# Layer 1 of a two-layer graph network: node sums carried on TensorE by an identity product and copied by ScalarE, one-hots split between VectorE and ScalarE

## The reference

```python
h = jnp.maximum(_layernorm(x), 0.0)
h = (h @ W).reshape(n, 4, 64)
h_l, h_r = (a_l * h).sum(-1), (a_r * h).sum(-1)
e = h_l[row] + h_r[col]
e = jnp.where(e > 0, e, 0.2 * e)
m = segment_max(e, row)
ex = jnp.exp(e - m[row])
att = ex / (segment_sum(ex, row)[row] + 1e-16)
out = segment_sum(att[:, :, None] * h[col], row)
```

## Time and profile before

| | |
|---|---|
| time, median of three runs | 2322.39 us |
| profiled execution: its time, its span | 2321.69 us, 2319.9 us |
| busy share over the span: PE, DVE, ACT, POOL | 85%, 77%, 64%, 61% |
| granted TensorE clock, mean | 0.944 |
| layer 1: first and last maximum (L1297) | 1565.5 us and 2279.1 us |
| layer 1, 560 us from its middle: PE, DVE, ACT, POOL busy | 440.89, 509.18, 368.04, 380.02 us |

### The profile page before, as it was taken

The page is one execution under the profiler, slowest core; times in us unless marked ns, Lnnn a source line. Parts: engine busy times, 40 slices in busy tenths (PEclk is TensorE's granted clock), DMA queues, the critical chain, the costliest instruction groups (busy, mean ns, idle before and its releaser), DMA issues.

```text
span 2319.9 us, 42068 instructions
## 1 busy us (share of the span) xinstructions
PE 1961.0 (85%) x9839; PEld 1426.4 (61%) x9840; DVE 1784.6 (77%) x4372; ACT 1479.1 (64%) x5220; POOL 1409.6 (61%) x1393
## 2 busy tenths in 40 slices
PE   5999999999958899998988889837777877877874
PEld 3777777777747677777777777624444444544542
DVE  5655444444359999998999999667999989999987
ACT  1585555555567777777777777446666666666660
POOL 0377777666776666665666664247666666666660
PEclk9999999999989999999999999977999989998997
DMA  8534444333389888888889882034433333343311
GB/s 279 160 133 144 157 146 146 138 138 131 113 291 301 299 290 292 298 293 280 296 290 308 291 296 76 19 93 113 110 107 107 105 108 100 105 110 104 106 32 56
DMA packets 162185, 403.69 MB, mean 174 GB/s; under 512 B 46887, under 2 KB 59099, under 8 KB 162108
## 3 DMA queue, kind: packets, MB, share of 16 engines
q0 software_dynamic: 79360, 276.09, 36.8%
q1 hardware_dynamic: 82748, 126.67, 17.4%
HBM read 343.89 MB, written 84.72 MB: 185 GB/s over the span
## 4 chain that ended last, share of the span: by engine, by line
PE 39%; DVE 28%; issue 16%; DMA 8%; ACT 4%; DVEq 4%; POOL 2%; SPq 0%; ACTq 0%; POOLq 0%
PE ps L1405 15%; DMA arena<-sorted_edges 6%; DVE gmx L1297 5%; PE ps L1391 4%; PE ps L1518 3%; PE ps L1521 3%; DVE arena L1329 3%; PE ps L1456 3%; PE ps L1533 2%; DVE work L1292 2%; DVE sc L1139 2%; DVE arena L1125 2%; DVEq L350 2%; PE ps L1643 2%; DVE arena L1132 2%
## 5 line engine op out<-in xcount | busy, mean ns | idle before, releaser
L630 POOL DMA_INDIRECT arena<-node_row,idxC x464 | 485.6, 1047 | 233.2 <-issue 136.8
L563 POOL DMA_INDIRECT sorted_edges<-work,pos_i x416 | 405.5, 975 | 236.5 <-issue 118.9
L1405 PE MATMUL ps<-w_sb,arena 128*128 128x256 f32 x1664 | 388.7, 386 | 0.2 <-ACT arena L674 0.2
L1643 PE MATMUL ps<-arena,hq 128*128 128x260 f32 x928 | 279.3, 428 | 96.2 <-DVE work L1292 92.8
L1069 DVE TENSOR_TENSOR work<-ps,b_bc 128x512 f32<-128x512 f32 x208 | 143.6, 691 | 273.6 <-PE ps L1405 273.6
L1405 PEld LDWEIGHTS ps<-w_sb,arena 128*128 128x128 f32 x1664 | 307.5, 190 | 72.2 <-issue 32.5
L585 POOL DMA_INDIRECT work<-node_kvx,idxB x232 | 245.7, 1059 | 154.4 <-DVE arena L1156 54.2
L585 POOL DMA_INDIRECT arena<-node_kvx,idxB x232 | 244.1, 1052 | 144.2 <-issue 51.2
L684 ACT ACTIVATE work<-work 128x256 f32<-128x256 f32 x416 | 187.5, 500 | 209.5 <-DVE work L1069 209.4
L1518 PE MATMUL ps<-arena,work 128*128 128x256 f32 x928 | 256.5, 400 | 59.1 <-issue 52.1
L1297 DVE TENSOR_REDUCE gmx<-ps 128x4 f32<-128x1024 f32 x232 | 282.5, 1218 | 28.4 <-PE ps L1618 28.4
(11 more groups left out here) (216 smaller groups left out, 3786.1 us busy)
## 6 DMA issues: line engine op xcount, KB each, us to landing
arena<-sorted_edges SPq DMA_DIRECT2D x232, 260.0 KB, 4.7
work<-sorted_rows SPq DMA_DIRECT2D x58, 256.0 KB, 3.6
arena<-in_edge_attr SPq DMA_DIRECT2D x25, 512.0 KB
node_kvx<-arena SPq DMA_DIRECT2D x24, 384.0 KB, 2.5
arena<-node_row,idxC POOLq DMA_INDIRECT x464, 3.3
sorted_edges<-work,pos_i POOLq DMA_INDIRECT x416, 2.5
sorted_edges<-arena SPq DMA_DIRECT2D x25, 260.0 KB
sorted_edges<-arena SPq DMA_DIRECT2D x1, 6240.0 KB
```

The lines of the kernel that those rows point to most:

```text
L563: pool.indirect_dma_start(rec_dram[:, :], bass.IndirectOffsetOnAxis(ap=pos_i[:, 4 * q + c:4 * q + c + 1], axis=0), recA[:, q % 8, c, :], N ...
L630: pool.indirect_dma_start(row1_g[:, st.slot(16), j, :], None, row1_dram[:, :], bass.IndirectOffsetOnAxis(ap=idxC[:, batch(st).slot(4), st. ...
L1405: ins = pe.matmul(ps[:, 5 + t, half * H:(half + 1) * H], hidT[:, r, m, half, t * P:(t + 1) * P], w2_sb[:, m, :], start=m == 0, stop=m == 1)
L1643: ins = pe.matmul(agg1[r], oneh1[:, r16, j, :], msg1[:, r, j, :], start=j == 0, stop=j == GJ - 1)
```

## The change

PE ends each step's `agg1` with a third product, the identity times the tile's old sums, in the same PSUM group, so that the bank holds the new sums. ACT copies the bank back into `acc1`; for the last step of a batch it multiplies by the next batch's `mscale` on the way, one instruction for each of the 4 heads, with the factor read per node row. `mscale` becomes 1 where the next batch begins with another tile (`same`). DVE's addition and scaling go. DVE makes the second chunk's one-hot in one comparison (`is_equal`) and ACT the first chunk's alone, for a step four back. The message ring grows from 2 to 8 slots. The `tiles16` loads of DVE go; PE and ACT each get one every eight steps. `agg1` on PE moves from 13 to 15 steps back, ACT copies 17 back. `indices` on ACT gets a second wait, for the maxima of the batch two before, because DVE now reads the numbers that it overwrites. The memset of `hrT` moves behind a wait. Core of the diff:

```diff
         def layer1(st):                                     # ScalarE
+                if st.u % 8 == 0:
+                    act_tiles[17] = tiles16(ACT_ENGINE, st.k, 17, st.u // 8)
+                d = st.back(17)
+                if d.real():
+                    act.wait_ge(s("agg1_ready"), d.n + 1)
+                    to = acc1[:, bass.ds(act_tiles[17][st.u % 8], 1), :].rearrange("p a n -> p (a n)")
+                    if d.u % BG == BG - 1 and not d.end():
+                        k = batch(d).back(-1)
+                        act.wait_ge(s("mscale"), k.n + 1)
+                        for h in range(NH1):
+                            ins = act.activation(to[:, h * HE:(h + 1) * HE], agg1[d.slot(2)][:, h * HE:(h + 1) * HE],
+                                                 ACT.Copy, scale=mscale[:, k.slot(2), h:h + 1])
+                        ins.then_inc(s("acc1_done"), 1)
+                    else:
+                        act.copy(to, agg1[d.slot(2)]).then_inc(s("acc1_done"), 1)
                 c = st.back(2)                              # the hrT copy, as before
...
-                if st.real():
-                    act.wait_ge(s("srcC_ready"), b.n + 1)
-                    for j in range(GJ):
-                        act.activation(away[:, st.slot(2), j, :], iota1[:, :], ACT.Abs,
-                                       bias=srcC[:, b.slot(4), g, j:j + 1], scale=-1.0).then_inc(s("away1"), 1)
+                h = st.back(4)
+                if h.real():
+                    act.wait_ge(s("srcC_ready"), batch(h).n + 1)
+                    act.activation(away[:, h.slot(2), 0, :], iota1[:, :], ACT.Abs,
+                                   bias=srcC[:, batch(h).slot(4), h.u % BG, 0:1], scale=-1.0).then_inc(s("away1"), 1)
...
-                e = b.back(3)
-                if g == 0 and e.real():
+                e = b.back(2)
+                if g == 3 and e.real():
...
             def indices(f):
                     act.wait_ge(s("hrT_mm"), f.n * (BG // 2) - 3 * (BG // 2))
+                    act.wait_ge(s("gmax"), f.n * BG - 3 * BG)
...
         def layer1(st):                                     # VectorE
-                if st.u == 0:
-                    tiles[8] = tiles16(DVE, st.k, 11, 0)
-                c = st.back(11)
-                if c.real():
-                    acc = tile(acc1, tiles[8][st.u % 8])
...
-                    dve.tensor_tensor(acc, acc, agg1[c.slot(2)], ALU.add).then_inc(
-                        s("acc1_done"), 1)
                 if st.real():
+                    if not st.first(16):
+                        dve.wait_ge(s("msg1_used"), st.n - 15)
+                    dve.tensor_scalar(oneh1[:, st.slot(16), 1, :], iota1[:, :], srcC[:, b.slot(4), g, 1:2], None,
+                                      ALU.is_equal)
...
         def layer1(st):                                     # TensorE
-                d = st.back(13)
+                if st.u % 8 == 0:
+                    pe_tiles[15] = tiles16(PE, st.k, 15, st.u // 8)
+                d = st.back(15)
...
-                        ins = pe.matmul(agg1[r], oneh1[:, r16, j, :], msg1[:, r, j, :],
-                                        start=j == 0, stop=j == GJ - 1)
-                    ins.then_inc(s("agg1_ready"), 1)
+                        ins = pe.matmul(agg1[r], oneh1[:, r16, j, :], msg1(d)[:, j, :],
+                                        start=j == 0, stop=False)
+                    ins.then_inc(s("msg1_used"), 1)
+                    if not d.first(1):
+                        pe.wait_ge(s("acc1_done"), n)
+                    pe.matmul(agg1[r], ident[:, :],
+                              acc1[:, bass.ds(pe_tiles[15][st.u % 8], 1), :].rearrange("p a n -> p (a n)"),
+                              start=False, stop=True).then_inc(s("agg1_ready"), 1)
```

More of the change, by code:

```diff
@@ L38 @@
 AHEAD = 2
+FRONT = 32
 class Step:
@@ L56, in real, with end @@
         return not isinstance(self.k, int) or 0 <= self.n < self.total
+    def end(self):
+        return isinstance(self.k, int) and self.n == self.total - 1
     def first(self, count):
@@ L276, in gnn_kernel @@
                       for v in (NT * (H + HR), NT * (H + HR) + NB * ME))
+        at_same = NT * (H + HR) + 2 * NB * ME
+        same = work[:, at_same:at_same + NB]
         apart = carve(NB * ME * ME).rearrange("p (b e f) -> p b e f", b=NB, e=ME)
@@ L336, in alone @@
         def alone(eng):
[L339 removed]
+            eng.sem_inc(s("waited"), 1)
         def tiles_of(eng, k, lag, count=8):
             _, values = nc.values_load_multi_w_load_instructions(
[L344 removed]
+                gt_i[0:1, bass.ds(k * 8 + (FRONT - lag), count)], engines=(eng,), min_val=0, max_val=NT - 1,
                 skip_runtime_bounds_check_because="the table's values are bounded by the minimum with NT - 1")
@@ L350, in tiles16 @@
             _, values = nc.values_load_multi_w_load_instructions(
-                gt_i[0:1, bass.ds(k * 16 + (16 - lag + 8 * half), 8)], engines=(eng,), min_val=0, max_val=NT - 1,
+                gt_i[0:1, bass.ds(k * 16 + (FRONT - lag + 8 * half), 8)], engines=(eng,), min_val=0, max_val=NT - 1,
                 skip_runtime_bounds_check_because="the table's values are bounded by the minimum with NT - 1")
@@ L386, in heads_of, with msg1 @@
             return rows[:, st.slot(4), :].rearrange("p (h d) -> p h d", d=HE)[:, :, 0:HD1]
+        def msg1(st):
+            r = st.slot(8)
+            return msg1_low[:, r, :, :] if r < 4 else msg1_high[:, r - 4, :, :]
         def kvx_g(st):
@@ L804, in _ @@
             act.wait_ge(s("hr_parts"), 2)
+            act.wait_ge(s("same"), 1)
             act_tiles = {}
@@ L840, in layer1 @@
                     act.copy(hrT[0:PARTS, pair(c).slot(2), :], trh).then_inc(s("hrT"), 1)
-                if st.real():
-                    act.wait_ge(s("srcC_ready"), b.n + 1)
-                    for j in range(GJ):
-                        act.activation(away[:, st.slot(2), j, :], iota1[:, :], ACT.Abs,
-                                       bias=srcC[:, b.slot(4), g, j:j + 1], scale=-1.0).then_inc(s("away1"), 1)
[L846 to L849, removed]
+                h = st.back(4)
[3 more added lines that the diff above has]
+                                   bias=srcC[:, batch(h).slot(4), h.u % BG, 0:1], scale=-1.0).then_inc(s("away1"), 1)
+                    act.wait_ge(s("away1"), h.n + 1)
+                    if not h.first(16):
+                        act.wait_ge(s("msg1_used"), h.n - 15)
+                    act.activation(oneh1[:, h.slot(16), 0, :], away[:, h.slot(2), 0, :], ACT.Relu, bias=1.0,
                                    scale=-1.0).then_inc(s("oneh1"), 1)
@@ L871, in layer1 @@
                     act.wait_ge(s("mdiff"), e.n + 1)
[L872 to L876, removed]
+                    act.activation(mscale[:, r, :], mdiff[:, r, :], ACT.Exp,
+                                   scale=same[:, bass.ds(e.n, 1)]).then_inc(s("mscale"), 1)
+            run(act, NG, 16, 17, layer1)
         @block.vector
@@ L1236, in _ @@
             link(dve.tensor_copy(gt_y[:, :, 0], own[:, :, 0]))
+            dve.tensor_tensor(same[:, :], gt_x[:, :, 0], gt_y[:, :, 0], ALU.is_equal).then_inc(s("same"), 1)
             link(dve.tensor_tensor(apart[:, :, :, :], gt_y[:, :, :].unsqueeze(3).to_broadcast([P, NB, ME, ME]),
@@ L1326, in layer1 @@
                         dve.wait_ge(s("exp1"), batch(m).n + 1)
-                    if not m.first(2):
-                        dve.wait_ge(s("agg1_ready"), m.n - 1)
-                    dve.tensor_tensor(msg1[:, m.slot(2), :, :].rearrange("p c (h d) -> p c h d", d=HE),
+                    if not m.first(8):
+                        dve.wait_ge(s("msg1_used"), m.n - 7)
+                    dve.tensor_tensor(msg1(m).rearrange("p c (h d) -> p c h d", d=HE),
                                       row1_g[:, m.slot(16), :, 0:HR].rearrange("p c (h d) -> p c h d", d=HE),
```

37 lines of the change are left out of this document (14 added, 23 removed).

## The result

The changed kernel takes 2433.22 us (median of four runs, 2427.38 to 2437.66) against 2322.38 for the kernel before (median of four): ratio 1.0474, interval 1.0457 to 1.0491. Slower was forecast, by 93 us; it is 111. The profiled execution has a span of 2427.9 us against 2319.9 and a mean granted clock of 0.935 against 0.944. Of these 108 us, 99.6 lie between the first and the last maximum of layer 1, 4.3 ahead of it (1565.5 became 1569.8) and 4.1 behind it (40.8 became 44.9; the sums now lag two steps more, which would account for it but was not tested).

A forecast was written before the change was run, and what follows sets the result against it. A chain of waits through VectorE, ScalarE and TensorE was taken as the bound: 58 x (13.7 - 12.31) = 81 us plus 12 for the clock, 93 on 2321.7, giving 2415 us; 8 in 10 from 2325 to 2460.

The forecast's parts named there:

- The ring of waits through three engines: Layer 1: ScalarE's `indices` waits for VectorE's maximum, TensorE for ScalarE's copies, VectorE's maximum for TensorE's score product; 12.3 us a batch.
- The rival with VectorE as the bound: Layer 1: the wait in `indices` is met early, a batch takes 10.9 us, time 2240; chance 0.13 for 2230 to 2310.
- R: End of the last maximum of batch b-2 on VectorE, which releases ScalarE's `indices` at the first step of batch b.
- the chain's 5.4: Second step's maximum can start at R + 5.4 us after TensorE's score product; VectorE itself would be ready at R + 4.4.
- the period: Time from one R to the next in a batch without register loads: 12.3 us, VectorE's saving of 1.4 taken back by waits.
- Four scaled copies: ScalarE's copies of 65 columns out of PSUM at a batch's edge: 0.25 us each, 1.0 together, ends 0.6 and 1.2.
- The hand-overs: Passing from one engine to the next along the chain, such as maximum to `indices`: 0.05 us each.
- VectorE alone at 10.9: VectorE's own need per batch in layer 1 without the chain's waits: 12.31 - 2.25 + 0.8 = 10.9 us.
- The loads: Register loads every second batch: ScalarE's adds 1.0 us, TensorE's 1.9 ahead of the sums; R at 15.1, or 13.6 with TensorE's at 0.
- the sign looked for: In layer 1 TensorE would idle ahead of the sums for "issue" every eighth step, because of its register load.
- the prediction's rival: Register loads cost nothing on the chain: 2321 us, 2333 with the clock, 2336 by the skill's floor; chance 0.12 for 2310 to 2350.
- The clock: TensorE's 3.9 us on the chain takes twice as long at 1.2 GHz, a sixth of the time: 12 us, bounds 0 and 38.

The follow-up runs named there:

- the filler: Changed kernel plus sixteen unneeded bf16 products on TensorE ahead of the sums at each batch's edge: 2396.32 us, ratio 1.0314 to the kernel before.
- the last three runs: Kernel before with the second wait in `indices` alone (2404.23 us), with `ew` and `mscale` moved too (2367.44), and with `indices` at the second step's end instead (2325.14).
- the ring open: Changed kernel with `indices` moved to the end of a batch's second step: 2304.04 us; with ScalarE's new register load also at the head of the step: 2325.92.

## Why the prediction was right, and where it was off

**What bounds the kernel after.** Right. The ring of waits through three engines is shown from both sides: the wait moved away takes 129 us off, the wait alone costs the kernel before 82, and moved back it costs nothing there. The rival with VectorE as the bound fell by its own test: its point was the second maximum at R + 4.4 against the chain's 5.4, and it starts at R + 5.6.

**The chain's terms.** R to the third maximum 7.9 forecast, 8.05 measured; the period 12.3 (the terms as written, 7.9 and 4.3, add up to 12.2) against 12.36 to 12.47 at 2.4 GHz. Four scaled copies were priced at 1.0 from start to start, between 0.6 and 1.2, with no row of their own; they take 0.8 (1787.99 to 1788.77). The hand-overs, priced at 0.05, were dearer: 0.13 from the maximum's end to `indices`. VectorE alone at 10.9: plain batches with VectorE ahead take 10.5 and 10.9.

**The loads.** ScalarE's was forecast from the earlier trace rows as 1.0 more behind `onehT1`: 1.06 idle there. TensorE's from the earlier trace rows as 1.9: here the sum was mis-sized. The load itself takes 1.94, but score product and spreading run beside a part of it. With the clock held the sums stand idle 0.6 to 1.5, mostly 0.9 or 1.5, and the load is worth 1.0 in a load batch where the prediction put 15.1 - 13.6 = 1.5. The two figures that the prediction gave for a load batch, 15.1 with TensorE's load and 13.6 without, are measured as 14.95 and 13.97. In the changed kernel itself the gap did not show, since the score product ahead of it ran at half speed and covered it: the sign looked for (sums waiting for "issue") was absent, though its reason was right.

The Trainium skill, "TensorE: Matmul & The Clock Gate" (table of specifications), gives TensorE a queue of 64. That the load could by this be issued early is borne out: it goes out with product and spreading still to run. That it would then be hidden is not: 1.94 is longer than what runs beside it, and there are 20 gaps in 20 load batches. (The prediction counts 28 instructions ahead of the load; the timeline has 18 matmuls and as many weight loads.) The Trainium skill, "DMA: Bandwidth & Descriptors" (latency and other measured facts), puts the floor of a register load at about 0.6; the loads here take 1.76 and 1.94. By that floor's batch of 12.6 the prediction's rival would stand at 2339, not 2336.

**The clock.** This is the term that failed: "Bounds 0 and 38, I take 12". The batches of the changed kernel take 14.5 and those with the filler 13.68; 0.8 a batch, and the filler gives 37 us back in spite of its own work, which is next to the upper bound. The prediction spread the old share of low clock over the chain evenly. What the rows show is that TensorE's idle time at a batch's edge became 3.5 in a load batch (the sums' longest wait before was 2.7) and that what follows runs at 1.2 GHz (identity product 1.23 in place of 0.70, sums 2.08 in place of 1.04), which is where the chain runs on TensorE. Waits that the chain itself makes lower the clock at the worst place.

**The sum.** 81 for chain and loads, 12 for the clock. From first to last maximum the filler's kernel needs 777.8 us, 64.2 more than before: in the middle of the layer its mean batch is the forecast's 13.7, but the first ten batches and the last three are on average shorter (12.7), which the prediction, with 58 equal batches, didn't see. The 35.4 that are missing to the changed kernel's 813.1 go to the clock, as far as the filler can tell, and 8.4 lie outside the maxima, also not foreseen: 64.2 + 35.4 + 8.4 = 108. Of the 8.4, the 4.3 ahead of layer 1 may be scatter: the last three runs change nothing there, and their first maxima lie at 1563.5, 1562.9 and 1569.8. So the nearness of 2415 to 2433 owes something to two errors of opposite sign (17 too much, 32 too little).

**Open.** Load batches of the changed kernel come in two kinds, 15.0 and 16.6. Half of the difference stays when the clock is held (14.56 and 15.33), and there the longer kind is the one in which TensorE's loop turns. The rest was not settled, nor why the plain batch behind the longer one has a low stretch of its own: about the same idle time (3.46 and 3.56) is followed by 3 us at 1.2 GHz in the one and by 6 in the other. Why the first ten batches are shorter stays open too.

## What to carry to other kernels

When a change adds a wait, first list what stands behind it on its engine and who needs each of these; the same wait costs 3.5% at the head of a step, where the engine must stand and wait, and nothing at the end of the next step, where it is already met. Then ask which waits of the new chain leave TensorE idle, and price the chain behind them at the lower clock. An early place for a register load isn't always a better one: with the ring open it cost 22 us less behind the long `onehT1`, which covers a part of it, than at the head of the step.

## What the runs showed of the hardware that was not expected

Sixteen products that compute nothing needed made the program 37 us faster (2396.32 against 2433.22), by keeping the granted clock in the middle of the layer at 0.99 in place of 0.89. A register load of eight tile numbers takes 1.76 us on ScalarE and 1.94 on TensorE. On ScalarE it shows as 1.06 us of idle time behind an instruction of 1.06, and as 1.6 to 2.2 behind short ones: here only the instruction just ahead covered it. On TensorE, which issues it with 0.8 to 1.3 us of matmuls still to run, mostly 0.9 or 1.5 are left.
